# The last half of the last expert: up products together, then down products one 128-row chunk at a time

## What is computed

```
def _L0_ffn_ref(x, Wr, W1, b1, W2, b2):
    xt = x.reshape(N, D)                                    # N = 4096, D = 256
    scores = jax.nn.softmax(xt @ Wr, axis=-1)
    G, idx = jax.lax.top_k(scores.T, k)                     # E = 8 experts, k = 1024 tokens each
    X_in = xt[idx]
    h = jax.nn.gelu(jnp.einsum('ekd,edh->ekh', X_in, W1) + b1[:, None, :], approximate=False)
    X_e = jnp.einsum('ekh,ehd->ekd', h, W2) + b2[:, None, :]
    contrib = (G[..., None] * X_e).reshape(E * k, D)
    out = jnp.zeros((N, D), dtype=x.dtype).at[idx.reshape(-1)].add(contrib)
```

## Time and profile before

| | before |
|---|---|
| median of 3 runs | 1247.35 us (1247.23 to 1248.04) |
| the profiled execution's own time | 1245.86 us |
| its span in the profile | 1243.9 us |
| PE busy | 1121.2 us (90%) |
| DVE, ACT, POOL busy | 827.7, 691.5, 818.1 us |
| mean granted TensorE clock | 0.966 |

### The profile page before, as it was taken

How to read it: one execution, slowest core, us unless ns; L and a number is a source line. 1 busy time by engine, 2 the same in 40 slices (tenths; PEclk the granted TensorE clock), 3 DMA queues, 4 the chain that set the end, 5 groups by cost and what they waited for, 6 DMA issues and landing times. The chain is left out here.

```text
span 1243.9 us, 19983 instructions
## 1 busy us (share of the span) xinstructions
PE 1121.2 (90%) x6999; PEld 982.9 (79%) x6999; DVE 827.7 (67%) x1958; ACT 691.5 (56%) x1434; POOL 818.1 (66%) x890
## 2 busy tenths in 40 slices
PE   3899999999999999999999988028999999999995
PEld 2788888888878878888888873017999999999994
DVE  4777787787887887887877856864555554463531
ACT  4666657656666666666666654005455555555542
POOL 3797897887887887987978841024474574664325
PEclk9999999999999999999999999559999999999997
DMA  5000110110100100100100003311452443533213
GB/s 190 1 18 1 39 31 1 39 31 1 44 26 1 44 26 1 43 27 35 31 5 35 18 1 107 106 30 49 111 125 35 115 109 42 125 71 71 30 17 34
DMA packets 42211, 58.09 MB, mean 47 GB/s; under 512 B 8897, under 2 KB 34945, under 8 KB 41985
## 3 DMA queue, kind: packets, MB, share of 16 engines
q0 software_dynamic: 13824, 21.24, 9.6%
q1 hardware_dynamic: 28288, 35.58, 8.6%
HBM read 35.71 MB, written 16.91 MB: 42 GB/s over the span
## 5 line engine op out<-in xcount | busy, mean ns | idle before, releaser
L1088 DVE TENSOR_TENSOR hT_lo<-hid,hT_hi 128x512 fp32r<-128x512 f32 x128 | 89.4, 699 | 179.5 <-ACT hT_hi L1228 179.5
L198 POOL TENSOR_SCALAR prob<-prob,row_inv 128x512 f32<-128x512 f32 (+3 forms) x256 | 134.6, 537 | 69.3 <-DVE row_inv L418 67.6
L1226 ACT ACTIVATE hid<-up,b_e 128x512 f32<-128x512 f32 x128 | 88.1, 688 | 155.2 <-PE up L1328 143.9
L272 ACT ACTIVATE prob<-prob,row_min 128x512 f32<-128x512 f32 (+3 forms) x256 | 142.4, 556 | 40.2 <-DVE row_min L411 39.4
L864 POOL DMA_INDIRECT x<-routed_rows,tokens x64 | 84.5, 1321 | 113.5 <-DVE tokens L1082 96.2
L354 DVE TENSOR_TENSOR pT_lo<-bank,pT_hi 128x384 fp32r<-128x384 f32 (+1 forms) x192 | 114.3, 595 | 42.3 <-ACT pT_hi L254 42.3
L875 POOL TENSOR_SCALAR y<-y,gate 128x256 f32<-128x256 f32 x64 | 33.8, 540 | 135.0 <-issue 134.2
L411 DVE CUSTOM_DVE_ANT_0 prob<-bank,mask_row 128x512 f32<-128x512 f32 (+3 forms) x256 | 114.1, 483 | 0.0
L884 POOL DMA_INDIRECT out<-y,tokens x64 | 102.3, 1598 | 17.3 <-issue 14.8
L206 POOL TENSOR_TENSOR q_sin<-q_sin,rope_t 128x512 f32<-128x512 f32 x64 | 82.4, 1287 | 44.1 <-ACT q_sin L296 42.3
L600 PE MATMUL bank<-ident,prob 128*128 128x128 f32 x640 | 101.7, 273 | 5.5 <-POOL prob L198 5.5
(11 more groups left out here) (196 smaller groups left out, 3808.0 us busy)
## 6 DMA issues: line engine op xcount, KB each, us to landing
raw<-in_w SPq DMA_DIRECT2D x16, 1024.0 KB, 8.6
emb_res<-emb SPq DMA_DIRECT2D x8, 512.0 KB, 3.7
out<-h SPq DMA_DIRECT2D x8, 512.0 KB, 2.9
routed_rows<-x SPq DMA_DIRECT2D x8, 512.0 KB, 3.2
x<-in_wq SPq DMA_DIRECT2D x1, 1024.0 KB, 5.3
x<-in_wk SPq DMA_DIRECT2D x1, 1024.0 KB, 5.0
x<-in_wv SPq DMA_DIRECT2D x1, 1024.0 KB, 7.2
x<-in_wo SPq DMA_DIRECT2D x1, 1024.0 KB, 10.0
```

The lines of the kernel that those rows point to most:

```text
L198: nc.gpsimd.tensor_scalar(pr, pr, row_inv[:, h % 2, k:k + 1], 1.0, ALU.mult, ALU.mult).then_inc(s["norm_done"], 1)
L272: nc.scalar.activation(pr, pr, ACT.Exp, bias=row_min[:, h % 2, k:k + 1], scale=-1.0, accum_out=row_sum[:, h % 2, k:k + 1]).then_inc(s["exp ...
L1088: nc.vector.tensor_tensor(out, in_, hi.bitcast(F32), ALU.subtract)\
L1226: nc.scalar.activation(hid[:, t % 2, :], up_ps[t % 2][:], ACT.Gelu, bias=bias)
```

## The change

For the second half of expert 7 only:

- PE runs the `up` products of steps 10 to 15 without `down` products between them. Then come all 96 `down` matmuls, ordered by chunk: for chunk c the 24 matmuls over all 8 blocks, in a PSUM bank of its own (`last_ps`: the two banks of `y_ps[1]`, `x_ps`, `l_ps`).
- The hidden blocks of steps 12 to 15 go to `xT[0]` instead of the ring (`hT_at`), since the ring's four slots hold steps 8 to 11 until the end.
- DVE adds the bias of a chunk when its 24 matmuls are done and multiplies by the gate itself.
- GpSimd no longer multiplies in this half; it issues each chunk's scatter when that chunk's gate is done.

```
+        last_ps = [*y_ps[1], x_ps, l_ps]
+        def hT_at(part, e, t):
+
+            if e == E - 1 and t >= DT + RING:
+                return xT[0][part][:].rearrange("p k (h n) -> p (k h) n", n=HALF)[:, t - DT - RING, :]
+            return hT[part][:, t % RING, :]
@@ gpsimd
             experts(pool, body)
-            add(E - 1, 1, 1)
+            for c in range(TB):
+                pool.wait_ge(s["last_gated"], c + 1)
+                alone(pool)
+                pool.indirect_dma_start(a["out"][:, :],
+                                        bass.IndirectOffsetOnAxis(
+                                            tokens[E - 1][:, TB + c:TB + c + 1], 0),
+                                        y[1][:, c, :], None, compute_op=ALU.add)\
+                    .then_inc(s["added1"], 16)
@@ vector
             experts(dve, body)
-            results(E - 1, 1)
+            after(dve, "added1", 16 * TB * (E - 1))
+            for c in range(TB):
+                dve.wait_ge(s["last_down"], c + 1)
+                nc.vector.tensor_tensor(y[1][:, c, :], last_ps[c][:, 0:M], b2[:, E - 1, :], ALU.add)\
+                    .then_inc(s["last_b2"], 1)
+                dve.wait_ge(s["last_b2"], c + 1)
+                nc.vector.tensor_scalar(y[1][:, c, :], y[1][:, c, :], gate[1][:, TB + c:TB + c + 1], None,
+                                        ALU.mult).then_inc(s["last_gated"], 1)
@@ scalar
-                    after(act, "down_done", k - (RING - 1))
-                    nc.scalar.activation(hT[0][:, t % RING, :], up_ps[t % 2][:], ACT.Gelu,
+                    if e < E - 1 or t < DT + RING:
+                        after(act, "down_done", k - (RING - 1))
+                    nc.scalar.activation(hT_at(0, e, t), up_ps[t % 2][:], ACT.Gelu,
                                          bias=bias).then_inc(s["h_hi"], 1)
@@ tensor
                     up(e, i, t)
+                    if e == E - 1 and t >= DT + LAG:
+                        continue
                     if t >= LAG:
                         down(e, i, t - LAG)
@@
             experts(pe, body)
-            for t in range(LAG):
-                down(E - 1, 1, STEPS + t - LAG)
+            e = E - 1
+            after(pe, "y_b2", e * 4)
+            for c in range(TB):
+                for dt in range(DT):
+                    t = DT + dt
+                    if c == 0:
+                        after(pe, "h_lo", e * STEPS + t + 1)
+                    for n, (x, z) in enumerate(PARTS):
+                        last = nc.tensor.matmul(last_ps[c][:, 0:M],
+                                                hT_at(x, e, t)[:, c * P:(c + 1) * P], w2[1][z][:, dt, :],
+                                                start=dt == 0 and n == 0,
+                                                stop=dt == DT - 1 and n == 2)
+                last.then_inc(s["last_down"], 1)
```

More of the change, by code:

```diff
@@ L778, in build_middle @@
             w_hi0 raw_in w_hi2 w_lo2 up_done down_done h_hi h_lo e_xt_tr e_xt_hi e_xt_lo hot_ready listed
-            tok_ready rows_in00 rows_in01 rows_in10 rows_in11 gate_ready y_b2 y_gated added0 added1 l_chain e_apart""".split()
+            tok_ready rows_in00 rows_in01 rows_in10 rows_in11 gate_ready y_b2 y_gated last_down last_b2 last_gated added0 added1 l_chain e_apart""".split()
         s = {n: ctx.enter_context(nc.semaphore(n)) for n in names} | shared
@@ L801, in experts @@
                 body(e, e % 2, e + 1 < E, e + 2 < E)
-        def wide(x):
-            return x.unsqueeze(2).to_broadcast([P, E, NB])
+        def hT_at(part, e, t):
+            if e == E - 1 and t >= DT + RING:
+                return xT[0][part][:].rearrange("p k (h n) -> p (k h) n", n=HALF)[:, t - DT - RING, :]
+            return hT[part][:, t % RING, :]
         @block.sync
@@ L1149, in body @@
                     after(dve, "h_hi", k + 1)
-                    low(hT[1][:, t % RING, :], hid[:, t % 2, :],
-                        hT[0][:, t % RING, :], "h_lo")
+                    low(hT_at(1, e, t), hid[:, t % 2, :], hT_at(0, e, t), "h_lo")
                     if t == LAG and not (isinstance(e, int) and e == 0):
```

## The result

The changed kernel takes 1240.92 us (median of 5 runs, 1239.33 to 1241.38) against 1247.35 us before: ratio 0.9946, 95% interval 0.9935 to 0.9956, so 6.4 us less (by the interval 5.5 to 8.1). The profiled execution went from 1245.86 to 1239.33 us and its span from 1243.9 to 1237.4.

The account below looks back on a forecast made before the run. Bound: a serial tail of 15.28 us behind a saturated PE. A new tail of 7.74 us (-7.54) and PE +0.45 gave -7.1, so 1247.35 to 1240.3 us; range 1239.0 to 1241.9.

Parts of the forecast that it names:

- The tail behind PE: From the last matmul to the end of the span: 7.74 us against 15.28 before, so -7.54.
- gate: VectorE's gate product of a chunk, SBUF to SBUF: 0.29 us, taken from the nearest row, with 0.42 as upper bound.
- start of the scatter: Last chunk's gate end to its scatter's start on waiting GpSimd: 0.85 us, bounds 0.20 and 0.95.
- PE: Up products together in steps 10 to 15: last matmul 0.45 us later, at 1229.07; bounds +0.1 and +1.0.
- The two waits: PE waits for a free up bank at steps 12 and 14: 0.11 us wait plus 0.11 restart each.
- 0.3 to spare: In chunk 0, 21 down matmuls cover the wait for step 15's low part, with 0.3 us left.
- GpSimd: First half's last scatter ends at 1223.23; last half's start near 1223.5, 1225.4, 1227.9, 1230.7; chunk 3's has 1.2 us slack.
- Rival 1: GpSimd's scatter issues and VectorE's gates hold each other up in the last half: 1241.1 to 1241.8 us; chance 0.15.
- Rival 2: Scatters are bound by the DMA engines, not their issue, so earlier issue moves nothing: about 1247 us; chance 0.03.
- Rival 3: PE's clock falls in the up steps' waits, 96 down matmuls run at 1.2 GHz: 1251.7 us; chance 0.02.
- The total: Whole kernel: tail -7.54 and PE +0.45, net -7.1 us, to a median of 1240.3 us.
- my sum's own range: Total with terms at their bounds: 1239.3 us below, 1241.1 above with the PE bound and a gate of 0.42.

Follow-up runs that it names:

- Run 3: The changed kernel with the last chunk's gate product on GpSimd instead of VectorE; 1240.93 us, ratio 0.9949 to the kernel before.
- run 4: The changed kernel with two more PSUM banks for the up products of steps 12 and 13; 1239.95 us, ratio 0.994 to the kernel before.
- run 9: The changed kernel measured again, unchanged, on one chip with a fused version; 1238.99 us, ratio 0.9938 to the kernel before.
- run 5: The changed kernel with down products of hidden blocks 0 to 3 kept between up products, only blocks 4 to 7 chunk by chunk; 1241.03 us, ratio 0.9956.
- run 6: The changed kernel with down products of hidden blocks 0 and 1 kept between up products, blocks 2 to 7 chunk by chunk; 1240.40 us, ratio 0.9946.
- run 7: The changed kernel with one more VectorE product of 128x1024 behind the gates of chunks 0 to 2; 1239.67 us, ratio 0.9941 to the kernel before.
- run 1: The changed kernel, but VectorE waits for all four chunks before starting chunk 0's bias; 1246.05 us, ratio 0.9987 to the kernel before.
- run 2: The kernel before, PE's order kept, with bias and gate on VectorE and a scatter chunk by chunk behind the last matmul; 1245.43 us, ratio 0.9982.

## Why the prediction was right, step by step

- **The tail behind PE**, 7.74 us predicted, 7.78 measured. Its terms: bias 0.42 (0.42); gate 0.29 (0.35, between the nearest row and the bound); start of the scatter 0.85 (0.80); from there to the end 6.10 (6.13). The gate's 0.06 too much and the start-up's 0.05 too little cancel, which is luck. The point that a GpSimd DMA pays where a GpSimd product doesn't was right. The reason I gave for it, that the start-up "hid behind the gates", was only half of it: it hid because the DMA's own wait was released by the first of four gates. Run 3 put one gate back in front and the 0.80 stayed, since it counts from the wait's release.
- **PE**, +0.45 predicted, +0.54 measured. The two waits are there, at the steps named, and run 4 removes them for 0.47. The other 0.07 is the down matmuls: from 1217.94 to 1229.33 they stand 0.1199 apart instead of 0.1193. That isn't the change: in run 9, the same kernel, they stand 0.1186 apart and PE is done at 20.38. Chunk 0 had no wait. It had 0.3 to spare, and runs 5 and 6 show what happens with fewer matmuls as cover.
- **GpSimd**: the first half's last scatter ended at 1224.23, 1.0 later than I had it; 0.46 of that is the later start of the stretch, the rest its gates (2.55 instead of 2.28) and its first scatter (1.83 instead of 1.58), which lie beside `low` instructions that now come closer together (that these are the cause is likely, but not tested). The slack took it. I had chunk 2's scatter 0.9 behind its gate and free of the queue; it was 0.79 behind it.
- **Rival 1** (mutual interference): real, but 0.29 for a scatter beside VectorE's products (run 7) and up to 0.50 beside `low` (the first half's last scatter took 2.06 in run 6). In the changed kernel itself chunk 0's scatter took 1.60 and the other three 1.56, far below the 1.5 in sum at which it would count. Its bound of 1.0 for each was not the highest that could be read, as gathers of L864 took up to 2.89 before instead of 0.94; no scatter came near that. **Rival 2** (DMA engines): excluded by run 1. **Rival 3** (the clock): the granted clock is 1.00, the 2.4 GHz level, through the waits, as the windows of the changed kernel show (columns as in the earlier trace rows, the clock in the third column from the end):

```profile
1208.60:1217.50 8.90, 8.90 (x41) 6.61 (x40) 4.75 (x7) 6.37 (x11) 3.26 (x5) 1.00 0.00 0
1217.50:1229.10 11.60, 11.60 (x97) 11.51 (x96) 3.82 (x8) 1.77 (x3) 9.67 (x7) 1.00 0.58 61
```

- **The total**: -7.1 predicted; the stretch gave -6.96, the medians -6.4 in the first comparison and -8.1 in the second (run 9). The 95% intervals of both, 5.5 to 8.1 and 6.1 to 9.5, hold the 7; the last section shows where the runs part ahead of the change. That the 1.49 between the profiled execution and the median, which I carried over, came out as 1.59 is luck: in run 9 it was 0.35. The upper end of my sum's own range, 1241.1, is 0.1 to 0.2 too high for the two terms that I named there (0.55 for PE, 0.13 for the gate: 1240.9 to 1241.0).

In shares of the stretch's 6.96: run 1 stands 1.29 under before (1.97 from bias and gate chunk by chunk on VectorE by run 2, less 0.52 for PE's order; of the other 0.16, 0.10 lies behind the last scatter's start, 6.15 against 6.05, which is the spread of all runs), and the overlap that this order allows gives the other 5.67.

## What to carry to other kernels

When the last thing that a kernel does is a serial chain behind a saturated engine, reorder that engine's last work so that outputs are complete one after another, and let each one's post-processing lie beside the next one's products. The spacing of the outputs should be at least the slowest stage's time per output (here 1.87 us of scatter issue; in run 5, at 1.4, they queued). And count the other side: products taken out from between others also covered waits there, here two banks' release (0.47 us) and the last block's low part (nothing at 21 matmuls of cover, a visible wait at 15 and at 9).

## What the runs showed of the hardware that I had not expected

- An indirect DMA on GpSimd starts 0.80 us after the release of its own wait, even if a GpSimd product released it and GpSimd was busy until then (0.79 in run 3), or 0.30 after the DMA ahead of it, whichever is later. A GpSimd product starts 0.1 to 0.2 after its release.
- The same code ahead of the change ends at different times from run to run. Attention's last VectorE instruction stood at 745.46 before and at 747.09 in run 6, the routing's copy of the transposed scores (VectorE too) at 777.16 and at 780.64, step 10 at 1208.64 and 1212.04. So 1.9 of the 3.4 us arise between the first two of these. From 745 to 780 the windows show a granted clock of 0.96 before and of 0.92 in run 6:

```profile
745.00:780.00 35.00, 28.99 (x142) 13.71 (x143) 20.48 (x43) 13.21 (x21) 3.71 (x54) 0.92 0.29 95
```

  But these windows don't hold the same code. Between those two instructions themselves the granted clock is 1.00 before (31.70 us) and 0.91 in run 6 (33.55 us). In both, PE then stands for 2.3 us, with the clock at 1.00 until then. After it the same 16 transposes and 4 routing products take 3.74 us before, the latter 1.88 at 1.00, and 5.40 in run 6, the latter 3.11 at 0.60. That is 1.66 of the 1.9; the two transposes of the scores are the rest (0.48 at 1.00 before, 0.68 at 0.50, the 1.2 GHz level, in run 6). In runs 3 and 7 these 4 products took 2.90 and 2.76, in all others 1.88, and these three runs have the latest step 10 (1210.63, 1210.30 and 1212.04, the others 1209.91 at most). So this part goes with the clock. Why it was granted less in some executions, and the 1.6 us that run 6 had lost ahead of 745, stay open. Such differences are why two kernels that differ by 0.7 us in the stretch can't be told apart by medians of five runs.
